# Expert weights as bf16 copies in DRAM, loaded through ACT's DMA queue, and three gathers placed ahead of one load

## The reference, cut to what matters

```
xn = layernorm(x)                                       # x: (4, 4096, 1024)
q, k, v = xn @ Wq, xn @ Wk, xn @ Wv;  g = log_sigmoid(xn @ Wgk1 @ Wgk2 + bgk2) / 16
o  = gated_linear_attention(q, k, v, g)                 # 4 heads, a state per head
a  = (rmsnorm(o) * rms_w * silu(xn @ Wg)) @ Wo
top2, w = top_k(xn @ gate_W + gate_b, 2), softmax       # 4 experts, 2 for each token
expert_e(t) = ln(relu(ln(t @ W1[e] + b1[e]) * g1 + be1) @ W2[e] + b2[e]) * g2 + be2
out = x + a + (xn + sum over the 2 experts of w * expert_e(xn))
```

## Time and profile before

| | us |
|---|---|
| median of 3 runs | 1229.83 (1229.48 to 1233.1) |
| the profiled execution | 1224.82 |
| its span on core 2, the slowest | 1223.0 |
| spans of cores 0, 2, 4, 6 | 1219.8, 1223.0, 1218.2, 1214.0 |
| spans of cores 1, 3, 5, 7 | 1217.8, 1215.3, 1199.2, 1197.8 |
| PE busy | 1012.3 (83%) |
| DVE busy | 613.4 (50%) |
| ACT busy | 537.9 (44%) |
| POOL busy | 224.8 (18%) |

### The profile page before, as it was taken

The page is one execution under the profiler, slowest core; times in us unless marked ns, Lnnn a source line. Parts: engine busy times, 40 slices in busy tenths (PEclk is TensorE's granted clock), DMA queues, the critical chain, the costliest instruction groups (busy, mean ns, idle before and its releaser), DMA issues.

```text
span 1223.0 us, 21526 instructions; the slowest of 8 cores (1197.8 to 1223.0 us)
## 1 busy us (share of the span) xinstructions
PE 1012.3 (83%) x4822; PEld 437.1 (36%) x4822; DVE 613.4 (50%) x1259; ACT 537.9 (44%) x1128; POOL 224.8 (18%) x271
## 2 busy tenths in 40 slices
PE   1598986789878977899868989997399999969983
PEld 1233333434333433343323433343144444424431
DVE  2314773643466346652675512114277777646762
ACT  3235344443543434354322111124277677747772
POOL 6000000000000000001023443014044332312221
PEclk9999997899999989999878999998699999989996
DMA  9996133412331242314533999978889967655744
GB/s 211 162 200 110 44 78 83 87 42 60 78 78 44 69 112 64 67 36 84 107 78 100 274 323 226 256 193 134 142 139 192 167 117 135 122 100 96 133 73 64
DMA packets 164301, 149.26 MB, mean 122 GB/s; under 512 B 119580, under 2 KB 131916, under 8 KB 164144
## 3 DMA queue, kind: packets, MB, share of 16 engines
q0 software_dynamic: 40624, 84.55, 37.3%
q1 hardware_dynamic: 120960, 53.76, 20.2%
q10 hardware_dynamic: 2592, 9.44, 2.4%
HBM read 111.58 MB, written 44.93 MB: 128 GB/s over the span
## 4 chain that ended last, share of the span: by engine, by line
PE 49%; DMA 13%; issue 12%; ACT 12%; DVE 10%; POOL 1%; DVEq 1%; SPq 1%; ACTq 0%; POOLq 0%; another core or an unknown queue 0%
PE pb L453 35%; PE pb L1625 13%; DMA s_xr<-x_tm 5%; ACT s_hT L1709 3%; DMA out<-zpad 2%; DMA s_xgT<-s_xg 2%; DMA s_xg<-xn_d,s_list 2%; ACT s_z L1733 2%; DVE s_L L982 2%; DMA out<-s_xr 1%; DVE s_W L1107 1%; PE pb L458 1%; SPq L467 1%; ACT s_sq L1113 1%; DVEq L135 1%
## 5 line engine op out<-in xcount | busy, mean ns | idle before, releaser
L1625 PE MATMUL pb<-s_we,s_xgT 128*128 x624 | 148.7, 394 | 37.2 <-DMA s_xgT<-s_xg 19.1
L453 PE MATMUL pb<-s_wv,s_xnT 128*128 128x512 bf16 x576 | 147.0, 404 | 23.2 <-ACT s_L L975 9.3
L1625 PE MATMUL pb<-s_we,s_hT 128*128 x624 | 149.7, 383 | 0.0
L453 PE MATMUL pb<-s_wo,s_ogl 128*128 128x512 bf16 x576 | 133.8, 387 | 9.1 <-issue 3.5
L453 PE MATMUL pb<-s_wg,s_xnT 128*128 128x512 bf16 x576 | 130.1, 383 | 5.5 <-DVE s_wb L964 5.3
L1107 DVE SCALAR_TENSOR_TENSOR s_W<-s_W,s_eb,pb 128x512 bf16<-128x512 bf16 x144 | 100.9, 742 | 51.6 <-PE pb L453 50.2
L1709 ACT ACTIVATE s_hT<-pb,s_gbs 128x128 bf16<-128x128 bf16 x312 | 116.4, 458 | 5.2 <-PE pb L458 3.9
L1745 POOL DMA_INDIRECT out<-s_y,s_list x39 | 61.7, 1582 | 255.5 <-DVE s_rf L1670 185.1
L1625 PEld LDWEIGHTS pb<-s_we,s_xgT 128*128 128x128 bf16 x624 | 61.7, 100 | 115.9 <-issue 57.2
L1733 ACT ACTIVATE s_z<-pb,s_rf 128x512 bf16<-128x512 f32 x78 | 56.4, 773 | 99.2 <-DVE s_rf L1670 93.1
L1113 ACT ACTIVATE s_sq<-pb 128x512 bf16<-128x512 f32 x72 | 42.9, 596 | 125.1 <-PE pb L453 86.6
(11 more groups left out here) (181 smaller groups left out, 1295.3 us busy)
## 6 DMA issues: line engine op xcount, KB each, us to landing
s_we<-W POOLq DMA_DIRECT2D x64, 256.0 KB, 19.8
s_xr<-x_tm ACTq DMA_DIRECT2D x18, 512.0 KB, 7.4
out<-s_xr SPq DMA_DIRECT2D x18, 512.0 KB
s_ogl<-og_d SPq DMA_DIRECT2D x16, 512.0 KB
s_x<-x_tm POOLq DMA_DIRECT2D x12, 512.0 KB, 6.0
og_d<-s_ogT POOLq DMA_DIRECT2D x12, 512.0 KB
s_wg<-Wg POOLq DMA_DIRECT2D x4, 1024.0 KB, 40.8
s_wv<-Wv POOLq DMA_DIRECT2D x4, 1024.0 KB, 67.3
```

What stands on the lines that cost most here:

```text
L453: lambda e: e.matmul(out=out, lhsT=lhsT, rhs=rhs, start=start, stop=stop),
L1625: t = P.emit("tensor", lambda e, dc=dc: e.matmul(out=ps, lhsT=lhs[:, dc, :], rhs=P.window("tensor", e, ("w", s, hf), s_we[layer][dc], 512) ...
```

## The change

Three things. (1) `cast_e(i)` copies a quarter of one weight matrix (256 rows, 1.05 MB of f32 to 0.52 MB of bf16) from DRAM to a new DRAM tensor `wb_d`; 32 such copies, two ahead of each unit from unit 4 on, on POOL's queue. (2) `load_e` now reads `wb_d` and is issued by ACT, not by POOL: expert 0 at the same place in the program, expert 1 at tile 6 of the projection with a wait for the end of attention (`att_done`), expert 2 in four parts ahead of tiles 9 to 12, expert 3 in four parts in steps 0 to 3. (3) The gathers of tiles 4 to 6 stand on POOL's list ahead of `load_vec(2, ...)`, not behind it in steps 1 to 3.

```diff
@@ -278,6 +278,7 @@
 
     xn_d = dt("xn_d", [T + 128, D], BF16).ap()
     og_d = dt("og_d", [NB * H * 128, 2048], BF16).ap()
+    wb_d = dt("wb_d", [2 * NE * D, D], BF16).ap()
     list_d = dt("list_d", [128 * 64, 2], I32).ap()
 
     arena = nc.alloc_sbuf_tensor("arena", [128, 207 * KB], mybir.dt.uint8)
@@ -1396,16 +1397,24 @@
 
 
     d_e = [mksem(f"d_e{e}") for e in range(NE)]
-
+    d_wb = [mksem(f"d_wb{e}") for e in range(NE)]
     k_e = [(d_e[e], 16 * 16) for e in range(NE)]
 
+    def cast_e(i):
+
+        n = D // 4
+        e, l, q = i // 8, i // 4 % 2, i % 4
+        gdma(wb_d[i * n:(i + 1) * n, :], (W1, W2)[l][e, q * n:(q + 1) * n, :], d_wb[e])
+
     def load_e(e, wait, part=range(16)):
-        o = e_off[e] // 2
         for i in part:
             l, dc = i // NDC, i % NDC
-            gdma(s_we[l][dc].ap[:, o:o + D],
-                 (W1, W2)[l][e, dc * 128:(dc + 1) * 128, :], d_e[e],
-                 wait=wait if i == 0 else [])
+            row = (2 * e + l) * D + dc * 128
+            P.emit("scalar", lambda x, l=l, dc=dc, row=row: x.dma_start(
+                out=s_we[l][dc].ap[:, e_off[e] // 2:e_off[e] // 2 + D],
+                in_=wb_d[row:row + 128, :]),
+                wait=(list(wait) + [(d_wb[e], 8 * 16)]) if i == part[0] else [], inc=d_e[e],
+                inck=16)
 
     d_vec = [mksem(f"d_vec{i}") for i in range(3)]
     k_vec = [None] * 3
@@ -1462,6 +1471,9 @@
                 side = [lambda: load_ogl(1), lambda: scale_wo(0), lambda: scale_wo(1)]
             elif h == 3:
                 side = [lambda: scale_wo(2), lambda: scale_wo(3)]
+            if b:
+                cast_e(2 * u - 8)
+                cast_e(2 * u - 7)
             unit(u, side)
             if h == 0 and b + 1 < NB and TILES[b + 1] == 4:
                 m_load(t0 + 2)
@@ -1554,7 +1566,9 @@
             if q == 6:
                 load_ogl(4)
                 load_vec(0, s_b1, b1b, att_done + [wo_te[(2, 3)], ogl_tok[3]])
-                load_e(1, [])
+                load_e(1, att_done)
+            if 9 <= q < 13:
+                load_e(2, att_done, range(4 * q - 36, 4 * q - 32))
             if q == 10:
                 P.branch(lambda: None, lambda: load_ogl(0))
             wo_head(q)
@@ -1749,13 +1763,13 @@
             inck=16)
 
     load_b2(att_done)
+    for s in range(4, 7):
+        f_gather(s)
     load_vec(2, s_g2, g2b, wo_done)
     def step(s, n):
 
-        if s < 4:
-            load_e(2, [], range(4 * s, 4 * s + 4))
         own, th = s < n, 1 <= s <= n
-        if 4 <= s + 3 < n:
+        if 7 <= s + 3 < n:
             f_gather(s + 3)
         if 4 <= s + 2 < n:
             f_xpose(s + 2)
@@ -1783,9 +1797,8 @@
         if 2 <= s < n + 2:
             f_z2(s - 2)
             f_stats2(s - 2)
-        if s >= 4:
-            load_e(3, [], range(2 * s - 8, min(2 * s - 6, 16)))
-
+        if s < 4:
+            load_e(3, wo_done, range(4 * s, 4 * s + 4))
     def rest(n):
 
         for s in range(SB - 3, SB):
```

## The result

| | before | after |
|---|---|---|
| median us of the slowest core | 1229.65 (1227.22 to 1233.1, 4 runs) | 1257.61 (1244.83 to 1330.2, 4 runs) |
| ratio, 95% interval | | 1.0204 [1.0161, 1.0247] |
| profiled execution, its span | 1224.8, 1223.0 | 1256.7, 1254.7 (core 4) |

The change made the kernel 28 us slower; 1223 was forecast, with 1240 as the top of the range. (Medians take in now and then a disturbed run, as the 1330.2 here; ratios leave these out.)

A forecast was written before the change was run, and what follows sets the result against it. PE was held mainly by a 19.1 us wait for `s_xgT` at the experts' start, then by a slowed projection. Terms -21.4 - 6 + 16.9 + 2 + 1 + 1 = -6.5 us took 1229.8 to 1223, range 1209 to 1240.

The forecast's parts named there:

- A: Start of the experts: gathers of tiles 4 to 6 ahead of g2 remove PE's wait for `s_xgT`, -21.4 us.
- B: Projection: halved weight reads of experts 0 and 1 lighten the traffic, -6 us (0 to -8.6).
- C: Start of the projection: expert 0's weights ahead of the residual loads on ACT's queue make PE stand, +16.9 us.
- D: Projection and expert steps 0 to 3: ACT issues 64 weight transfers, +2 us (0 to 8.6).
- E: Projection: expert 1 ahead of tile 7's residual, expert 2 ahead of those of tiles 10 to 13, +1 us (0 to 10).
- third rival: Projection: residual tiles held longer, at SP's queue's rate; C 23, tile 7 delayed 11 us; sum +12, 1241 us; chance 0.20.
- F: Attention: the 32 casting copies are almost hidden, +1 us (0 to 8).
- fifth rival: Attention pays for the copies, F at 8 us: sum +0.5, 1230 us; chance 0.06.

The follow-up runs named there:

- x1: Kernel before with only the gathers of tiles 4 to 6 moved ahead of g2's load: 1218.33 us, ratio 0.9901; repeated, 1211.49 us, 0.9873.
- x3: Changed kernel with the bf16 weights issued on POOL's queue and not ACT's: 1224.23 us, ratio 0.9976 to the kernel before.
- x12: Changed kernel with expert 1's weights alone on POOL's queue, the other experts' on ACT's: 1243.77 us, ratio 1.0112 to the kernel before.
- x2: Kernel before with the 32 casting copies added and never read: 1276.79 us median of six runs, ratio 1.0194.
- x6_again: The files of x6_after_T run a second time: 1204.76 us, ratio 0.9819 to the kernel before.
- x6_after_T: x3 with the casting copies moved to the middle of each unit, waiting for the transposes issued so far: 1220.5 us, ratio 0.986 to the kernel before.
- x7_both: x6_after_T with the rows of `wb_d` also padded by 64 elements: 1207.48 us, ratio 0.9827 to the kernel before.
- x11_placed_act: Changed kernel with copies in mid-unit, waiting for the unit's transposes, all weights still on ACT's queue: 1235.67 us, ratio 1.0054 to the kernel before.
- x5: x3 with `wb_d` rows padded by 64 elements, so a copy is 256 rows and not 16 long pieces: 1221.31 us, ratio 0.9937 to the kernel before.

## Why the prediction was wrong

**A was right in place, too large alone.** The wait of the earlier trace rows is gone, as said. Experts to the end fell by 18.3 us against 21.4. By x1 and its repeat the gathers give 13; with the bf16 loads as well it is 20.5 (x3) and 18.3 (after). That the lighter or earlier weights give the rest is the likely reading, not one that a kernel isolated.

**B was right**: -5.7 against -6 in tiles 4 to 8, and -3.2 more behind tile 12, where x3 has none of it (51.6).

**C was right in mechanism, and in size with some luck**: +16.2 against +16.9. The first weight's issue to the tile took 19.4 us where 23.4 were forecast (689.3 - 665.93), and PE's waits for DVE's add are 12.7, 14.7, 8.5 and 10.8 us on cores 0, 2, 4 and 6, in the mean 11.6 where 14.5 were forecast. The slow restart adds 2.4, as forecast, and the wait for DVE's scaling of Wo just before (`s_wo`) grew by 1.9, which the sum did not have. By the Trainium skill, "DMA: Bandwidth & Descriptors", section "Queues, rings and completion order", one row is consumed in order and rows take turns by packets; x3 and x12 agree, since the same 4.2 MB on POOL's queue leave tile 0 to 2 at 24.8 us (x3) and tile 8 to 9 at 7.9 (both).

**D cost nothing that shows in the experts.** Experts to the end take 373.8 to 377.3 us in the six profiled executions in which ACT issues expert 3 and 373.8 to 376.2 in the five in which POOL issues it from `wb_d`. In the projection the issues hold ACT (10.11 and 11.62 us for 16), and that time lies inside the wait for the tile they delay; at tile 8 it is about 5 us of the stall at most, by the estimate under x12_e1_pool.

**E is the first step that failed.** "Expert 1 takes 14.5 us with the tile behind it, but the residual loads run about two tiles (15.8 us) ahead once nothing is in their way: **+1** (0 to 10)." It measured +21.7. The lead was more than that: PE stopped at 796.18 - 17.49 = 778.7, 22 us after the first weight's issue. The 14.5 us was wrong: 37.2. I had taken the 0.32 MB for each microsecond of engine time as a rate by the clock, at a place where SP moves 2.1 MB of `s_ogl` and three stores, and had added SP's share in C but left it out in E. The share of 44.4% gives 34 us. The third rival named this and took 27 us from the earlier trace rows with a chance of 0.20, which was nearer. 37.2 - 22 leaves 15 us of late tile; with scaling and add PE waits 17.49 us, and with the slow restart the stretch is 21.7 longer in the mean of the cores.

**F is the second.** "No wait of PE there ends on a DMA. Cover: DVE's and ACT's own chain." with +1 (0 to 8). It measured +16.6 (x2: +14.4), twice the upper end; the fifth rival named attention, but with those 8 us and a chance of 0.06. Full engines for 88 us over 16 units was an average, and averages were not the trouble. The copies stand at the head of a unit, where SP issues the transposes that PE needs in that unit. Timeline of the changed kernel, core 4, head of a unit:

```profile
313.37 1.01 POOL L463 DMA_DIRECT2D wb_d<-W  x2
...
314.40 1.80 SPq L468 DMA_TRANSPOSE s_kdT<-s_kd  x1
...
316.35 24.80 SPq L468 DMA_TRANSPOSE s_xnT<-s_xtm  x2
...
319.46 1.07 POOL L463 DMA_DIRECT2D s_x<-x_tm  x2
320.52 1.01 POOL L463 DMA_DIRECT2D wb_d<-W  x2
...
352.16 1.01 PE L454 MATMUL pb<-s_v,s_kdT 128*128 128x512 bf16 x2 [15.72 <-DMA s_kdT<-s_kd]
```

The transpose that PE waits for is the one of 314.40, issued 1 us behind two copies and ahead of the `s_xnT` transposes that hold SP for 24.80 us. It was late on its way and not in SP's list. The chain of work that led to PE's restart, 300 to 356 us:

```profile
314.40 37.62 DMA s_kdT<-s_kd
```

The same holds for the other waits of this kind in the changed kernel: such a transpose, issued ahead of `s_xnT` with copies beside it, took 14.2 to 25.0 us. The DMA view of 316 to 341 us (its first line is the packet time in 40 slices, in tenths of 16 engines and cut at 9; issues end with the median us to landing):

```profile
DMA  0009930008999999799009200959900590059909
...
q0 software_dynamic: 467, 2.37, 76.4%
q1 hardware_dynamic: 1317, 0.33, 24.1%
...
wb_d<-W POOLq DMA_DIRECT2D x2, 512.0 KB, 27.9
...
s_xnT<-s_xtm SPq DMA_TRANSPOSE x2, 27.1
s_kdT<-s_kd SPq DMA_TRANSPOSE x1, 37.6
```

The packets of the two queues took 76.4 + 24.1 = 100.5% of the engines' time, yet only 108 GB/s were moved. The zeros of the first line are no idle engines: the view counts a packet's whole time where it starts. From 318 to 319 us it has 28 packets, half of them over 8 KB, with nearly three times the time that the 16 engines have in 1 us:

```profile
q0 software_dynamic: 28, 0.46, 293.5%
```

That is 2.935 x 16 / 14 = 3.4 us for each of the 14 large packets (0.46 / 14 = 0.033 MB), while a packet of the transposes carries 0.33 MB / 1317 = 250 bytes and took 0.241 x 16 x 25 / 1317 = 0.07 us. A small packet that has to wait for a large one again and again would be this slow; that is a likely reading and no run isolates it.

On core 4 in attention as a whole (230 to 640 us) the median `s_kdT` takes 9.9 us to land in the changed kernel and 5.1 in x6_again. That the place of the copies beside these transposes is the cause is shown: against x3, x6_after_T moves the copies behind them, with a wait, and changes nothing else, and 13.8 of x3's 17.9 us go (15.1 and 15.7 in x6_again and x7_both; 16.0 of 16.6 in x11_placed_act against the changed kernel). The eight kernels with the copies at the head of a unit start the projection at 672.5 to 683.0, the seven executions without copies or with placed ones at 661.1 to 666.2. How much is the long pieces is open: in x5 a copy is 272 packets and not 32 (POOL's queue has 1024 more in x2 than before for 32 copies, and 7680 more in x5 than in x3), the second wait is gone and the first stays. Two copies with little beside them (265 to 280 us) landed in 7.9 us.

Together: the two failed steps are worth 20.7 + 15.6 = 36.3 us against the 33.4 between -6.5 and +26.9; the others come to -2.9.

## What to carry to other kernels

Work out a transfer's time from its bytes at the queue's own rate divided by the share it will have at that place, and do so for every place at which it is moved in front of something that is waited for; the DMA view of a stretch gives both numbers. The 44.4% of this case was read afterwards; beforehand one has to add up what the other queues will move there. Give bulk loads a queue that carries nothing that the next few microseconds need: the bytes moved were the same in x3 and in the changed kernel, and the queue, with the engine that issues on it, was worth 2.3%. A new transfer in a part "with idle DMA engines" is hidden only if it does not meet the small transfers there that something waits for; place it behind them with a wait, and read their landing times, not the mean share.

## What the runs showed of the hardware

- ACT's queue moved 0.31 MB for each microsecond of engine time in both stretches, alone (84.2% of the engines) or beside others (44.4%). Its time by the clock doubled with the share.
- Issuing 16 transfers of 256 KB takes ACT 10.11 to 11.62 us, against 8.57 us on POOL; the one residual issue behind them took 1.15 us and not 0.34. A DMA transpose can hold SP's list far longer: 24.80 us for two beside casting copies.
- In the stretch with casting copies beside transposes the packets took 100.5% of the engines' time at 108 GB/s, against 94% at 280 GB/s in 692 to 712 us, and the transposes took 27.1 and 37.6 us to land. Full engines can mean few bytes.
